# Where 62 reflections of an eigensolver stand beside two layers of a graph network, and who ends the second layer's LSTM

## The chip, the cores and the metric

The kernel runs as one launch on one core of a Trainium2 chip. The metric is the device time of that core in microseconds (us). The engines are TensorE (PE in the profile), VectorE (DVE), ScalarE (ACT), GpSimd (POOL) and SyncE (SP), and they work at the same time, tied together by semaphores.

## What is computed

The state `x` is 128 graphs of 64 nodes with 128 features (8192 tokens). Four layers are added to it, each behind a layer norm and a relu, all over the same 64x64 adjacency `adj`:

```python
h = jnp.maximum(_layernorm(x, axis=-1), 0.0)
x = x + _L0_gnn_ref(h, adj, ...)   # aggregate, W1, batch norm, relu, W2, batch norm
h = jnp.maximum(_layernorm(x, axis=-1), 0.0)
x = x + _L1_gnn_ref(h, adj, ...)   # two graph products, then four LSTMs over windows of 1, 2, 3, 4 nodes
h = jnp.maximum(_layernorm(x, axis=-1), 0.0)
x = x + _L2_gnn_ref(h, adj, ...)   # U.T, W1, relu, W2, U; U = eigenvectors of the normalised Laplacian
h = jnp.maximum(_layernorm(x, axis=-1), 0.0)
x = x + _L3_gnn_ref(h, adj, adj, ...)
```

The third layer needs `_, U = jnp.linalg.eigh(L_norm)` of a 64x64 matrix that depends on `adj` alone. The second layer's LSTMs are run over all windows of a node sequence, `i, f, g, o` being the four gates:

```python
c = sigmoid(f) * c + sigmoid(i) * tanh(gg)
h = sigmoid(o) * tanh(c)
```

## The kernel before, in words

The tokens are laid out as 4 quarters (`ITER`) of 4 chunks (`NK`) of 512 columns. The stages in time are the first layer (its first pass over 16 chunks, then its second over 8 pairs), a lead-in of the second layer for quarter 0, the LSTM for quarters 0 to 3, and the third and fourth layers, interleaved.

The eigenvectors come from a Householder reduction to tridiagonal form in 62 reflections, then a search for eigenvalues on a grid (two rounds), then a scan for each eigenvector (the code's "twist"), then a few 64x64 products. All of that is a serial chain on VectorE, with one or two small products on TensorE in each link. It is spread beside the first two layers. A reflection beside the first layer is `reflection_beside_l0` (lines 1386 to 1432): VectorE writes two columns into `NI`, TensorE multiplies them (`row_product`), GpSimd takes a square root, VectorE goes on, TensorE multiplies `S` by `vcol` (`av_product`), VectorE updates `S`. One such reflection stands in every step of the first layer's loop from step `FIRST_REFLECTED` on. A reflection beside the LSTM is `reflection` (from line 1453): it needs no GpSimd, sets its vector at L1494, sends TensorE one `av_product` (`small_product`), and takes it up at L1507. What else VectorE does there (adding the first layer's and the LSTM's results to the state at L2110, adding a bias at L2041, and the layer norms) is put between the reflection's instructions. Each link's small operations are also given to generators called `beside`, which a reflection advances by one item at each of its waits.

Nothing is scheduled on the chip. TensorE's order in the LSTM is written by a planner that counts its own clock: after each product it checks whether the next small product is due, and puts it there. `PACE_AV` is the distance between two reflections' products in that clock, `PACE_GRID` that of the two grid rounds, `PACE_TWIST` that of the scan. `beside_norm` adds to the pace while a quarter's layer norm is on VectorE. The planner's times are a layout, not a measurement. Once an instruction stands in TensorE's queue it waits there for its semaphore, and all behind it wait too.

The LSTM of a quarter has 11 rounds (`LSTM`; p is the window, s the step in it): rounds 0 and 1 are p = 1, rounds 2 and 3 p = 2, rounds 4 to 6 p = 3, rounds 7 to 10 p = 4. Each round is done for two sets q = 0, 1 of 1024 tokens, so there are two half rounds. In a half round TensorE makes 3 or 4 gates of 512, 336 or 256 columns, ScalarE takes their sigmoids and tanh (L1061), GpSimd forms the products (L1205), ScalarE takes tanh of the cell (L1085) and GpSimd the last product. In the last quarter the rounds from `ON_VECTOR` on have their products on VectorE (`last_rounds`, L2128), which is free only once the eigenvectors are done. In the same quarter ScalarE normalises quarters 0 and 1 for the third layer (L973, four instructions for each chunk) in the half rounds that `LAST_NORMED` names, between the gates and the tanh of the cell. Their statistics are `last_stats`, 92 small instructions on VectorE from a point in the planner's clock on.

At step 23 of the first layer VectorE also makes the aggregation matrices of the LSTM layer (`BIASES_AT`, L1993 to L1998), six instructions in a row between two reflections.

## Time and profile before

| what | us |
|---|---|
| median of 3 runs (896.1 to 898.14) | 897.49 |
| the profiled execution itself | 898.26 |
| its span in the trace | 896.5 |
| first layer | 0 to 155 |
| lead-in of the LSTM layer | 155 to 186 |
| LSTM, four quarters | 186 to 608 |
| third and fourth layer | 608 to 896 |
| TensorE busy, whole span | 792.7 (88%) |
| VectorE busy, whole span | 577.7 (64%) |
| ScalarE busy, whole span | 505.6 (56%) |
| GpSimd busy, whole span | 330.9 (37%) |

A row of the timeline gives the start in us, the duration in us, the engine, the line of the kernel, the operation, out<-in, shapes, and in brackets the time that the engine was idle before it and what ended that. TensorE's records come in two for each fp32 matmul, so "x6" are three matmuls. TensorE waits with the weight load and with the matmul; the matmul's wait is the one counted here, unless it is said otherwise. In the program's order below a matmul is one row.

### The profile page before, as it was taken

The page shows a single profiled execution, that of the slowest core. Times are in us where ns is not written, and L with a number is a line of the kernel's source. Part 1 is how long each engine was busy: PE and PEld are TensorE (multiplying, and loading weights), DVE is VectorE, ACT ScalarE, POOL GpSimd, SP SyncE. Part 2 cuts the span into 40 slices and gives each one's busy share as a digit, 9 for nine tenths or more (in the row PEclk, how much of TensorE's full clock was granted, in tenths as well). Part 3 has the DMA queues.
Part 4 walks back from the last instruction along what each step waited for, and adds up shares of the span by engine and source line. Part 5 has one row for each costly group of instructions (what it writes and reads, how often), then busy time and mean ns, then how long its engine had stood idle before and what let it go on. Part 6 is the DMA issues. An engine that isn't in the chain of part 4 may idle for free.

```text
span 896.5 us, 15860 instructions
## 1 busy us (share of the span) xinstructions
PE 792.7 (88%) x5323; PEld 520.6 (58%) x5323; DVE 577.7 (64%) x3091; ACT 505.6 (56%) x958; POOL 330.9 (37%) x490
## 2 busy tenths in 40 slices
PE   3867687799999999999799859999899999999998
PEld 1444334654688556864467524676748748747646
DVE  3899878799789997889997996646710720700101
ACT  2676575575766765675655634684654464434531
POOL 3556201376456655567555635300410220200000
PEclk9999798799999999999999979999999999999999
DMA  8000000000000000000000000000000100100101
GB/s 358 12 1 1 0 0 1 1 0 1 1 1 1 1 2 0 2 0 1 0 1 1 1 0 1 1 0 2 3 1 2 49 1 1 49 1 1 50 0 48
DMA packets 3409, 13.49 MB, mean 15 GB/s; under 512 B 512, under 2 KB 512, under 8 KB 2688
## 3 DMA queue, kind: packets, MB, share of 16 engines
q1 hardware_dynamic: 3328, 12.48, 3.5%
q8 instruction: 42, 0.69, 0.3%
q14 instruction: 39, 0.32, 0.1%
HBM read 8.28 MB, written 4.19 MB: 14 GB/s over the span
## 4 chain that ended last, share of the span: by engine, by line
PE 57%; DVE 26%; ACT 8%; POOL 5%; issue 3%; DMA 0%; DVEq 0%; SPq 0%; ACTq 0%; POOLq 0%
PE PS L525 56%; POOL BIG L1205 2%; ACT BIG L1061 2%; ACT T L1027 2%; DVE ST L1914 2%; DVE Fq L1693 1%; DVE seg L1694 1%; ACT T L973 1%; DVE X L2110 1%; DVE PS L1575 1%; DVE PS L1577 1%; DVE Z L1582 1%; DVE Z L1579 1%; ACT BIG L1085 1%; POOL sc L1145 1%
## 5 line engine op out<-in xcount | busy, mean ns | idle before, releaser
L525 PE MATMUL PS<-BIG,wts 128*128 128x512 f32 (+2 forms) x952 | 337.6, 497 | 8.3 <-ACT BIG L1061 5.0
L1205 POOL TENSOR_TENSOR BIG<-BIG 128x256 f32<-128x256 f32 (+2 forms) x220 | 210.3, 965 | 144.3 <-ACT BIG L1061 80.2
L525 PEld LDWEIGHTS PS<-BIG,wts 128*128 128x128 f32 x952 | 175.5, 191 | 131.2 <-issue 97.6
L1061 ACT ACTIVATE BIG<-PS,lbias 128x256 f32<-128x256 f32 (+2 forms) x312 | 162.0, 560 | 93.0 <-PE PS L525 90.9
L525 PE MATMUL PS<-H,wts 128*128 128x256 f32 (+2 forms) x312 | 111.3, 485 | 10.8 <-POOL H L1205 5.6
L965 ACT ACTIVATE BIG<-PS 128x1024 f32<-128x1024 f32 x64 | 64.7, 1024 | 85.4 <-PE PS L525 85.0
L525 PE MATMUL PS<-T,wts 128*128 128x512 f32 x192 | 104.8, 670 | 2.9 <-ACT T L965 2.5
L2155 DVE COPY T<-PS 128x256 f32<-128x256 f32 x32 | 12.2, 419 | 135.1 <-PE PS L525 135.1
L965 ACT ACTIVATE T<-PS 128x512 f32<-128x512 f32 (+1 forms) x96 | 48.3, 523 | 69.9 <-PE PS L525 69.7
L973 ACT ACTIVATE T<-X,shift,rstd 128x128 f32<-128x128 f32 x192 | 78.6, 483 | 10.3 <-POOL shift L1182 9.5
L525 PEld LDWEIGHTS PS<-H,wts 128*128 128x128 f32 x312 | 56.6, 193 | 45.7 <-issue 20.1
L2110 DVE TENSOR_TENSOR X<-X,PS 128x512 f32<-128x512 f32 x64 | 41.9, 680 | 61.7 <-PE PS L525 56.1
L1153 POOL TENSOR_SCALAR rstd<-mv 128x4 f32<-128x4 f32 x28 | 6.4, 228 | 190.6 <-DVE mv L1897 190.5
L1085 ACT ACTIVATE BIG<-BIG 128x512 f32<-128x512 f32 (+2 forms) x88 | 44.8, 509 | 53.1 <-POOL BIG L1205 52.8
L525 PE MATMUL PS<-wts,T 128*128 128x128 f32 (+1 forms) x384 | 62.1, 315 | 0.5 <-DVE T L2155 0.2
L525 PEld LDWEIGHTS PS<-wts,T 128*128 128x128 f32 x384 | 55.9, 194 | 8.5 <-issue 3.2
L525 PEld LDWEIGHTS PS<-wts,BIG 128*128 128x128 f32 x512 | 57.8, 192 | 1.9 <-issue 1.9
L525 PE MATMUL PS<-wts,BIG 128*128 128x128 f32 x512 | 57.8, 275 | 0.0
L525 PEld LDWEIGHTS PS<-T,wts 128*128 128x128 f32 x192 | 36.0, 208 | 34.8 <-issue 28.1
L1145 POOL TENSOR_TENSOR sc<-sc,cst 128x1 f32<-128x1 f32 x25 | 13.7, 547 | 69.2 <-DVE sc L1401 69.2
L525 PEld LDWEIGHTS PS<-S,vcol 128*128 128x128 f32 x124 | 20.8, 201 | 30.8 <-DVE S L1416 26.9
L525 PE MATMUL PS<-S,vcol 128*128 128x64 f32 (+61 forms) x124 | 24.2, 275 | 13.2 <-DVE S L1416 13.1
(334 smaller groups left out, 1215.5 us busy)
## 6 DMA issues: line engine op xcount, KB each, us to landing
X<-x_in SPq DMA_DIRECT2D x4, 1024.0 KB, 16.4
out<-X SPq DMA_DIRECT2D x16, 256.0 KB, 2.2
wts<-w_in SPq DMA_DIRECT2D x1, 3542.0 KB, 13.4
cst<-cst_in SPq DMA_DIRECT2D x1, 419.0 KB, 3.4
AA<-adj_in SPq DMA_DIRECT2D x2, 16.0 KB, 1.9
```

Source lines behind the costliest of these rows:

```text
L525: return nc.tensor.matmul(o, l, r, start=start, stop=stop)
L965: nc.scalar.activation(dst, src, fn, **kw).then_inc(act_done[k], 1)
L973: j = nc.scalar.activation(to[:, k, t * P:(t + 1) * P], X[:, a:a + P], ACT.Relu, bias=shifted[:, k, t:t + 1], scale=scale[:, k, t:t + 1])
L1027: j = nc.scalar.activation(T0[:, k, t * P:(t + 1) * P], X[:, a:a + P], ACT.Relu, bias=shift[:, k, t:t + 1], scale=rstd[:, k, t:t + 1])
L1061: nc.scalar.activation(LB[:, q, {"i": I_, "g": G_, "f": F_, "o": O_}[g], 0:n], PS[:, 3 * q + rank[q] % 3, 0:n], ACT.Tanh if g == "g" else ...
L1085: nc.scalar.activation(LB[:, q, I_, 0:n], LB[:, q, CELL, 0:n], ACT.Tanh).then_inc(act_set[q], 1)
L1145: return nc.gpsimd.tensor_tensor(o, ap, mh[:, 0:1] if e is None else e, ALU.pow)
L1205: nc.gpsimd.tensor_tensor(out, a, b, op).then_inc(pool_set[q], 1)
L1575: gop(v.scalar_tensor_tensor(ta, xn, d[:, i:i + 1], Z[:, up, :], ALU.add, ALU.mult))
L1914: v.bn_stats(ST1[:, h, c, :], Y1[:, h, c * CH:(c + 1) * CH]).then_inc(hidden_seen, 1)
L2110: v.tensor_tensor(x, x, src, ALU.add).then_inc(dve_done[k], 1)
L2155: v.tensor_copy(*graph_half(k, 1, to, side)).then_inc(dve_done[k], 1)
```

## The change

- `FIRST_REFLECTED` goes from 3 to 7: the first layer's steps 3 to 6 have no reflection, and the LSTM gets 41 in place of 37.
- The LSTM's layout is written anew: `PACE_AV` 5.9 to 5.4, `PACE_GRID` 49.0 and 41.5 to 48.5 and 38.5, `PACE_TWIST` 33.0 to 40.0.
- The six instructions of step 23 become a generator of its own, two of them beside the reflection of each of the steps 21, 22 and 23.
- The statistics for the normalisation of quarter 0 get tiles of their own (`rstd0`, `shift0`) and are taken early, in quarter 1's LSTM beside the biases of quarter 2, where the pace is 0.4 longer for 36 us of the planner's clock. Those of quarter 1 stay late (from 30.0 in place of 24.0 behind the last graph product).
- `ON_VECTOR` goes from 6 to 8: in the last quarter GpSimd also makes the products of rounds 6 and 7.
- `LAST_NORMED` moves the eight normalisations from rounds 6 to 9 (one in each half round) to rounds 8 to 10 (two in each half of round 8, one in each half of 9 and 10).

```diff
-ON_VECTOR = 6
-LAST_NORMED = {(6, 0): [(0, 0)], (6, 1): [(0, 1)], (7, 0): [(0, 2)], (7, 1): [(0, 3)],
-               (8, 0): [(1, 0)], (8, 1): [(1, 1)], (9, 0): [(1, 2)], (9, 1): [(1, 3)]}
+ON_VECTOR = 8
+LAST_NORMED = {(8, 0): [(0, 0), (0, 1)], (8, 1): [(0, 2), (0, 3)],
+               (9, 0): [(1, 0)], (9, 1): [(1, 1)], (10, 0): [(1, 2)], (10, 1): [(1, 3)]}
...
-FIRST_REFLECTED = 3
+FIRST_REFLECTED = 7
...
-BIASES_AT = L0_FIRST + 4
+MATRICES_AT = [L0_FIRST + 2, L0_FIRST + 3, L0_FIRST + 4]
...
-PACE_AV = 5.9
-PACE_GRID = [49.0, 41.5]
-PACE_TWIST = 33.0
+PACE_AV = 5.4
+PACE_GRID = [48.5, 38.5]
+PACE_TWIST = 40.0
...
-NORM_BESIDE, NORM_LASTS, LAST_NORMS = 1.4, 20.0, 24.0
+NORM_BESIDE, NORM_LASTS, LAST_NORMS = 1.4, 20.0, 30.0
+NORM_0 = (0.4, 36.0)
...
-                return any((j, 1, "turn") in there and clock[0] < there.get((j, NK - 1, "turn"), clock[0]) + NORM_LASTS
-                           for j in range(1, ITER))
+                for j in range(1, ITER):
+                    if (j, 1, "turn") in there and clock[0] < there.get((j, NK - 1, "turn"), clock[0]) + NORM_LASTS:
+                        return NORM_BESIDE
+                    if j == 2 and (0, NK - 1, "turn_h") in there and clock[0] < there[0, NK - 1, "turn_h"] + NORM_0[1]:
+                        return NORM_0[0]
+                return 0.0
...
+            def lstm_matrices():
...
+                dve.wait_ge(ld_w, 16)
+                made(v.tensor_scalar(tmp[:, :], PS[:, 7, 0:P], TINY, None, ALU.max))
+                yield
+                dve.wait_ge(prep_dve, done[0])
+                made(v.reciprocal(tmp[:, :], tmp[:, :]))
+                yield
+                made(v.tensor_scalar(BDR[:, :], BDAT[:, :], c1(0), None, ALU.mult))
+                yield
+                made(v.tensor_scalar(RB1[:, :], PS[:, 7, 0:P], W("bg1"), None, ALU.mult))
+                yield
...
+                if n in MATRICES_AT:
+                    beside = beside + [itertools.islice(matrices, 2)]
...
-                        yield from biases(i + 1)
+                        early = iter(())
+                        if i == 1:
+                            early = last_norm(0, rstd0, shift0, [there[0, NK - 1, "turn_h"] + 2.0], NORM_0[1] / 46)
+                        yield from merged(early, biases(i + 1))
                     else:
-                        yield from merged(last_stats(), behind)
+                        late = last_norm(1, rstd3, shift3, [there[i, NK - 1, "agg2"] + LAST_NORMS], LN_STEP)
+                        yield from merged(late, behind)
```

`last_norm` is `last_stats` for one quarter: 16 statistics, 16 aggregations, the roots and 4 shifts.

The instructions move on three engines. The first place is TensorE's queue in the first layer, steps 1 to 6 (`BDHT` is the aggregation, `T,wts` the product with W1, `NI,S` and `S,vcol` the two products of a reflection). Before:

```order
L525 MATMUL PS<-BDHT,T 128x128 x4
L525 MATMUL PS<-NI,S 128x65
L525 MATMUL PS<-T,wts 128x512 x2
L525 MATMUL PS<-S,vcol 128x64
L525 MATMUL PS<-BDHT,T 128x128 x4
```

After:

```order
L529 MATMUL PS<-BDHT,T 128x128 x4
L529 MATMUL PS<-T,wts 128x512 x2
L529 MATMUL PS<-BDHT,T 128x128 x4
L529 MATMUL PS<-T,wts 128x512 x2
L529 MATMUL PS<-BDHT,T 128x128 x4
L529 MATMUL PS<-NI,S 128x65
```

Five products with W1 now come ahead of the first reflection's row product, of which the piece shows the last two; before, one did.

The second place is TensorE's queue between the second grid round (`sc,cst`) and the scan's product (`both_ways`), in the last two quarters (`BIG,wts` and `H,wts` are gates, `BDR,T` a graph product, `cst,BIG` a transpose of the LSTM's result). Before:

```order
L525 MATMUL PS<-sc,cst 128x1
L525 MATMUL PS<-BDR,T 128x128 x4
L525 MATMUL PS<-BIG,wts 128x256 x8
L525 MATMUL PS<-BDR,T 128x128 x4
L525 MATMUL PS<-BIG,wts 128x256 x16
L525 MATMUL PS<-H,wts 128x512 x18
L525 MATMUL PS<-both_ways,cst 128x128
```

After:

```order
L529 MATMUL PS<-BIG,wts 128x256 x8
L529 MATMUL PS<-BDR,T 128x128 x4
L529 MATMUL PS<-BIG,wts 128x256 x16
L529 MATMUL PS<-H,wts 128x512 x18
L727 MATMUL PS<-cst,BIG 128x128 x4
L529 MATMUL PS<-H,wts 128x512 x3
L529 MATMUL PS<-BIG,wts 128x512 x3
L529 MATMUL PS<-H,wts 128x512
L529 MATMUL PS<-BIG,wts 128x512
L529 MATMUL PS<-both_ways,cst 128x128
```

The scan's product now stands behind eight more gates of 512 columns and a transpose; one graph product fewer stands between it and the grid round.

The third place is ScalarE's queue in round 8 of the last quarter (`BIG<-PS,lbias` are the four gates, `T<-X,shift,rstd` a normalisation, `BIG<-BIG` the tanh of the cell). Before:

```order
L1061 ACTIVATE BIG<-PS,lbias 128x256 x4
L973 ACTIVATE T<-X,shift,rstd 128x128 x4
L1085 ACTIVATE BIG<-BIG 128x256
L1061 ACTIVATE BIG<-PS,lbias 128x256 x4
L973 ACTIVATE T<-X,shift,rstd 128x128 x4
L1085 ACTIVATE BIG<-BIG 128x256
```

After:

```order
L1069 ACTIVATE BIG<-PS,lbias 128x256 x4
L981 ACTIVATE T<-X,shift,rstd 128x128 x8
L1093 ACTIVATE BIG<-BIG 128x256
L1069 ACTIVATE BIG<-PS,lbias 128x256 x4
L981 ACTIVATE T<-X,shift,rstd 128x128 x8
L1093 ACTIVATE BIG<-BIG 128x256
```

Each half of round 8 now has two normalisations ahead of its tanh; rounds 6 and 7 have none, and round 10 has one in each half.

## Rows read from the trace of the kernel before

**Rows 1.** Timeline of PE in the first layer's first pass
```profile
40.56 0.43 PE L525 MATMUL PS<-NI,S 128*128 128x62 f32 x2 [0.94 <-DVE NI L1395]
40.83 1.94 PE L525 MATMUL PS<-T,wts 128*128 128x512 f32 x4
...
45.68 0.43 PE L525 MATMUL PS<-NI,S 128*128 128x61 f32 x2 [0.94 <-DVE NI L1395]
```

**Rows 2.** Timeline of ACT in the same steps
```profile
42.80 1.26 ACT L990 ACTIVATE BIG<-PS,wts 128x512 f32<-128x512 f32 x2 [0.94 <-PE PS L525]
44.78 0.60 ACT L965 ACTIVATE T<-PS 128x512 f32<-128x512 f32 x1 [0.72 <-PE PS L525]
```

**Rows 3.** Timeline of PE about step 23 of the first layer
```profile
128.46 0.42 PE L525 MATMUL PS<-NI,S 128*128 128x45 f32 x2 [2.60 <-DVE NI L1395]
128.70 4.52 PE L525 MATMUL PS<-T,wts 128*128 128x512 f32 x6
...
134.72 2.82 PE L525 MATMUL PS<-T,wts 128*128 128x512 f32 x6
```

**Rows 4.** Timeline of DVE there, the longest of the six
```profile
125.94 0.95 DVE L1994 RECIPROCAL tmp<-tmp 128x128 f32<-128x128 f32 x1
```

**Rows 5.** Instructions of L1512, one for each reflection but the last (min/median/max)
```profile
L1512 DVE SCALAR_TENSOR_TENSOR urow<-xrow,sc,PS x36: 200/226/244, 171.1 to 384.5; 128x37 f32<-128x37 f32 x1, 128x36 f32<-128x36 f32 x1, 128x35 f32<-128x35 f32 x1, 128x34 f32<-128x34 f32 x1
```

**Rows 6.** Waits of DVE, 186 to 391 us (total us, times, longest)
```profile
DVE sc L1507 <- PE PS L525: 15.6, 19, 2.5
```

**Rows 7.** Waits of PE's weight loads in the same stretch
```profile
PEld PS L525 <- DVE S L1494: 4.3, 8, 0.8
```

**Rows 8.** Timeline of DVE, the reflections' take-up of their products
```profile
199.76 0.21 DVE L1507 TENSOR_SCALAR sc<-PS,sc 128x1 f32<-128x1 f32 x1
...
227.53 0.22 DVE L1507 TENSOR_SCALAR sc<-PS,sc 128x1 f32<-128x1 f32 x1 [1.38 <-PE PS L525]
...
286.92 0.22 DVE L1507 TENSOR_SCALAR sc<-PS,sc 128x1 f32<-128x1 f32 x1 [0.67 <-PE PS L525]
...
292.11 0.22 DVE L1507 TENSOR_SCALAR sc<-PS,sc 128x1 f32<-128x1 f32 x1 [0.24 <-PE PS L525]
```

**Rows 9.** Timeline of DVE at the second grid round
```profile
489.80 0.22 DVE L1658 SCALAR_TENSOR_TENSOR sc<-PS,sc 128x1 f32<-128x1 f32 x1 [3.88 <-PE PS L525]
```

**Rows 10.** Timeline of PE at the scan's product
```profile
531.50 0.79 PE L525 MATMUL PS<-both_ways,cst 128*128 128x128 f32 x2 [8.79 <-DVE both_ways L1718]
...
532.94 4.04 PE L525 MATMUL PS<-H,wts 128*128 128x512 f32 x6
```

**Rows 11.** Timeline of ACT in rounds 8 to 10, last quarter
```profile
588.63 1.64 ACT L973 ACTIVATE T<-X,shift,rstd 128x128 f32<-128x128 f32 x4
590.17 0.40 ACT L1085 ACTIVATE BIG<-BIG 128x256 f32<-128x256 f32 x1
...
594.06 0.40 ACT L1085 ACTIVATE BIG<-BIG 128x256 f32<-128x256 f32 x1
...
604.27 0.42 ACT L1085 ACTIVATE BIG<-BIG 128x256 f32<-128x256 f32 x1
...
607.84 0.42 ACT L1085 ACTIVATE BIG<-BIG 128x256 f32<-128x256 f32 x1
```

**Rows 12.** Timeline of PE, round 7 of the last quarter
```profile
581.43 2.86 PE L525 MATMUL PS<-H,wts 128*128 128x256 f32 x12 [1.78 <-DVE H L2128]
...
587.09 0.70 PE L525 MATMUL PS<-H,wts 128*128 128x256 f32 x2 [1.26 <-ACT BIG L1061]
```

**Rows 13.** Timeline of POOL, products and how long they take
```profile
544.07 1.27 POOL L1205 TENSOR_TENSOR H<-BIG 128x512 f32<-128x512 f32 x1 [0.74 <-ACT BIG L1085]
...
570.75 0.90 POOL L1205 TENSOR_TENSOR BIG<-BIG 128x336 f32<-128x336 f32 x1 [0.59 <-ACT BIG L1085]
```

**Rows 14.** Timeline of DVE, one operation twice, beside POOL and not
```profile
544.34 1.04 DVE L1844 TENSOR_TENSOR lnv<-lnv 128x16 f32<-128x16 f32 x1
...
545.89 0.17 DVE L1844 TENSOR_TENSOR lnv<-lnv 128x16 f32<-128x16 f32 x1
```

More of the change, by code:

```diff
@@ L374, in build @@
         shift3 = sb("shift3", [P, NK, TPC])
+        rstd0 = sb("rstd0", [P, NK, TPC])
+        shift0 = sb("shift0", [P, NK, TPC])
         T0 = sb("T0", [P, NK, CH])
@@ L1082, in _ @@
                                 norm_tiles(j, k, "norm", j * NK + k + 1, C_PE.at(ITER - 1, "agg2"),
[L1083 removed]
+                                           *((T3, rstd3, shift3) if j else (T0, rstd0, shift0)), by=[last_norms] * NK)
                         act.wait_ge(pool_set[q], R_POOL.at(i, f"c{r}" if s else f"ig{r}"))
@@ L2048, in biases, with last_norm @@
                         bias(i, k)
-                def last_stats():
-                    at = [there[ITER - 1, NK - 1, "agg2"] + LAST_NORMS]
+                def last_norm(j, scale, to, at, step):
                     def later():
-                        busy(0.2)
-                        at[0] += LN_STEP
+                        busy(0.17)
+                        at[0] += step
                         return at[0]
                     for k in range(NK):
-                        dve.wait_ge(act_done[k], C_ACT.at(ITER - 1, "norm"))
-                    for j, scale, to in ((0, rstd, shift), (1, rstd3, shift3)):
-                        for k in range(NK):
-                            dve.wait_ge(dve_done[k], C_DVE.at(j, "add_h"))
-                            for t in range(TPC):
-                                a = j * SG + k * CH + t * P
-                                do(v.bn_stats(stats[:, k, t, :], X[:, a:a + P]))
-                                yield later()
-                        wait()
-                        for k in range(NK):
-                            for t in range(TPC):
-                                do(v.bn_aggr(mv[:, k, t, :], stats[:, k, t, :]))
-                                yield later()
-                        wait()
-                        yield from norm_roots(do, wait, later, scale)
-                        for k in range(NK):
-                            v.scalar_tensor_tensor(to[:, k, :], mv[:, k, :, 0], -1.0, scale[:, k, :], ALU.mult, ALU.mult)\
-                                .then_inc(last_norms, 1)
-                            yield later()
@@ new lines, in last_norm @@
+                        dve.wait_ge(dve_done[k], C_DVE.at(j, "add_h"))
+                        for t in range(TPC):
+                            a = j * SG + k * CH + t * P
+                            yield later()
+                            do(v.bn_stats(stats[:, k, t, :], X[:, a:a + P]))
+                    yield later()
+                    wait()
+                    for k in range(NK):
+                        for t in range(TPC):
+                            yield later()
+                            do(v.bn_aggr(mv[:, k, t, :], stats[:, k, t, :]))
@@ L2080, in first_add @@
+                    yield later()
+                    wait()
+                    yield from norm_roots(do, wait, later, scale)
+                    for k in range(NK):
+                        v.scalar_tensor_tensor(to[:, k, :], mv[:, k, :, 0], -1.0, scale[:, k, :], ALU.mult, ALU.mult)\
+                            .then_inc(last_norms, 1)
+                        yield later()
                 def first_add(k):
```

24 lines of the change are left out of this document (13 added, 11 removed).

## The prediction, written before the result

> **What bounds the kernel now.** I read stage by stage, since a busy share of the whole span mixes stages with different limits. In the first layer the timeline shows TensorE idle 0.94 us once in each step, waiting for VectorE's two columns of the next reflection, and the same row product comes again 5.12 us later [rows 1]: the step is paced by the reflection's chain. In the LSTM TensorE is nearly always busy, and the question is who of the two is late. Over the reflections VectorE waited 15.6 us for products that TensorE sent late [rows 6], and TensorE waited 4.3 us for VectorE [rows 7]. So there TensorE sets the end, with the chain close behind. At the scan it is the other way: TensorE stood 8.79 us with the scan's product at the head of its queue [rows 10]. In the last rounds ScalarE's normalisation stands between gates and tanh [rows 11], and TensorE waits for what follows from it [rows 12]. The third and fourth layers aren't touched.
>
> **First layer, steps 3 to 6.** Without a reflection a step goes around W1's product (1.94 us), ScalarE's copy of its result (1.26), ScalarE's copy of the next aggregation (0.60) and back to W1's product [rows 1, 2]: 3.80, with three or four hand-overs 3.95 us. The next aggregation on TensorE runs beside the first copy, and GpSimd's layer norm beside all of it. Against 5.12 us that is 1.17 less, in four steps **-4.7 us**. Ends: nothing less than 3.80 (-5.3), and one step in which TensorE's clock drops. Such a drop is seen at step 23: behind an idle time of 2.60 us six records took 4.52 us, and 2.82 us elsewhere [rows 3], 1.7 us more. In the short steps nothing would hide it (-3.0).
>
> **Step 23's matrices.** Six instructions in a row kept the reflection's columns back: TensorE waited 2.60 us, and the 1.7 us of slow clock came behind it [rows 3], less 0.2 us of wait that every step has: 4.1 us. Spread out two by two they still take VectorE's time, the reciprocal 0.95 us [rows 4] and five of 0.2 to 0.3 us, 2.2 us in all, and the reflection sets the step here too, so I count all of it. TensorE's gaps become short, and the slow clock should go: **-1.9 us** (between 0, if the clock still drops, and -4.1, if the slots hide them). The 21 reflections that stay are four elements longer, **+0.4 us**.
>
> **The LSTM: four more reflections, set closer.** Before, 36 take-ups lie between 171.1 and 384.5 us, 213.4 us for 35 intervals [rows 5]. Without its waits [rows 6] VectorE needed 197.8 us. Each more costs what a quiet one does, 292.11 - 286.92 - 0.24 = 4.95 us [rows 8], a little less beside other work: 4.9, and 19.6 for four. The norm of quarter 0, moved in here, costs what the norm of quarter 1 did: four intervals from 199.76 to 227.53, less 1.38 us of waiting [rows 8], are 26.4 us; less four reflections and one addition of 0.6 that leaves 6.2 us. VectorE's need becomes 197.8 + 19.6 + 6.2 = 223.6 us.
> TensorE's own time was 213.4 - 4.3 = 209.1 us. Counted in its order, the last of the 41 products stands behind 5.9 us more of matmuls than the last of the 37 did (1.2 us are the added small products, the rest LSTM). That is 215.0 us. So VectorE is 8.6 us late if it never idles. It will idle where TensorE is late anyway (2 to 3 us of the 15.6 are such places), so TensorE waits some 11 us, where it waited 4.3. With the added products themselves: **+6.8 and +1.2 us**. What each wait holds up is all of TensorE's queue, the gates first, and with them ScalarE and GpSimd. Bounds: +2 if VectorE hides half of it in the waits of the rounds (ScalarE and GpSimd are late there too), +11 if each interval falls badly.
>
> **Grid rounds.** The first is bound by VectorE before and after. In the second VectorE waited 3.88 us for its product [rows 9], which now comes 3.4 us earlier in TensorE's order: the slack is used up and nothing is gained. **0** (0 to +1).
>
> **The scan.** From the take-up at 489.80 [rows 9] to 531.50 [rows 10] VectorE worked 41.7 us, TensorE 41.7 - 8.8 = 32.9. In the new order TensorE has eight 512-column matmuls and a transpose more before the scan's product and a graph product less, at 0.86 us for one of 512 columns (2.82 us hold three, with the first one's start [rows 3]) 6.9 + 0.5 - 0.9 = 6.5 us: 39.4. VectorE has one addition (0.6) and some ten norm instructions (1.2) more: 43.5. The wait goes from 8.8 to 4.1: **-4.7 us**. Behind the wait six records took 4.04 us [rows 10], 1.2 more than the 2.82 of the same size [rows 3]; half of that should go, **-0.6**.
>
> **The last rounds.** The norms leave rounds 6 and 7, where TensorE waited 1.78 and 1.26 us [rows 12]: -3.0. GpSimd takes some 0.3 us longer for a product that the next round waits for (0.90 us for 336 columns [rows 13]), once or twice: +0.3. In round 8 a half takes gates, two norms of 1.64 us and a tanh of 0.40 on ScalarE. With one norm it took 594.06 - 590.17 = 3.89 us [rows 11]. ScalarE is full in it (four gates are about 1.7), so two make about 5.35: +2.9 for two halves. Round 10 had none and took 607.84 - 604.27 = 3.57 [rows 11]; one in each half adds 0.3, and the last stands ahead of the last tanh, for which the third layer waits: +1.7. Sum **+1.9 us**. The tail of small products has less norm work beside it: **-0.3**.
>
> **The sum.** First layer -4.7 - 1.9 + 0.4 = -6.2 us. LSTM 6.8 + 1.2 + 0 - 4.7 - 0.6 + 1.9 - 0.3 = +4.3 us. Together -1.9 us on the profiled execution's own 898.26, which is 0.8 above the median of the runs. I take 0.5 to 1 us off for waits that overlap: a TensorE that waits for VectorE lets ScalarE and GpSimd catch up, and their waits shrink. That is about -2.7 us, 895.6 on the profiled execution and **894.8 us** on the median of 897.49.
>
> **A rule against it.** One small operation took 1.04 us when it began beside a product of GpSimd that ran 1.27 us from 544.07, and 0.17 us two steps later [rows 13, 14]. The Trainium skill ("SBUF — State Buffer", section "Who interferes with whom") says that a VectorE instruction with two inputs in SBUF and a GpSimd instruction that reads SBUF block each other for a whole instruction, whoever starts first. The trace agrees in this pair. By that rule the moved norm's eleven two-input operations, in a stretch where GpSimd works, could each meet such a block: eleven times 0.87 us, 9.6 us in place of the 6.2 taken from the trace, and 3.4 us more in the sum.
>
> **The rivals.**
> *VectorE keeps up.* The reflections need about as much as before between products, because the waits for TensorE were spread where they can be used; TensorE's waits stay near 4 to 6 us. For it: 15.6 us of slack were there, and every single wait of TensorE was under 0.9 us [rows 6, 7]. Against it: the counts leave VectorE 8.6 us short. Then 4 to 6 us less than my sum, 889 to 891 us.
> *VectorE becomes the bound (slower).* One mechanism, in quarters 0 to 2 of the LSTM: additions, biases and norms fall on intervals with no slack, and each delay goes to TensorE's queue undiminished, because the next products are due at once. Price: intervals of 5.9 to 7 us against 5.3, in three norm stretches and three rows of additions, +11 us and over in place of 6.8, with the blocked operations on top +3; the scan still waits. It decides the sign once TensorE's waits for VectorE in the reflections pass about 14 us. 898 to 903, most likely 900.
> *The first layer gives little.* The clock drops in the short steps and at the matrices: 3 us of the 6.2 are lost, 897.5 us, no change.
>
> **Chances.** Forecast 0.45 (891.5 to 897), VectorE keeps up 0.2, VectorE the bound 0.2, little from the first layer 0.15. A measurement of this kernel can tell about 0.2%, 1.8 us, from no change. Below 895.7: the second case and most of the first, 0.56. Above 899.3: most of the third, 0.17. Between: 0.27. The range, 888.5 to 901 us, takes in the second case and most of the third.
>
> **What would show it.** First layer: W1's products 3.9 to 4.0 us apart in steps 3 to 6, and the layer over at 149 in place of 155 us. Step 23: no wait of 2.6 us and no 4.52 us. LSTM: TensorE's waits for the reflections' vector near 11 us with VectorE's waits for TensorE under 5 us. Scan: a wait of about 4 us. Round 8: tanh to tanh 5.3 us. The LSTM from its first product to its end some 3 to 4 us longer. The prediction is wrong if TensorE's waits in the reflections stay at 5 or go past 14, or if the clock falls in the short steps.

## The result, and the profile after

The changed kernel takes **908.07 us** (median, 907.40 to 912.86), the kernel before 896.80 on the same chip; the ratio is 1.0132, interval 1.0113 to 1.0151. It is 11.3 us slower where I forecast 2.7 us faster, and it lies outside the range. The first layer did better than forecast, the LSTM 15 us worse. The profiled execution is the slowest of the four, 4.8 us above the median; between the two traces lie 14.6 us, so some 3 us of what the rows below show are not in the medians.

**First layer.** The timeline of TensorE after, steps 2 to 6 (start, duration, engine, line, operation, out<-in, shapes, idle before and who ended it), answers to [rows 1]:

```profile
25.58 1.96 PE L529 MATMUL PS<-T,wts 128*128 128x512 f32 x4 [0.93 <-ACT T L973]
29.38 1.98 PE L529 MATMUL PS<-T,wts 128*128 128x512 f32 x4 [0.95 <-ACT T L973]
33.21 1.98 PE L529 MATMUL PS<-T,wts 128*128 128x512 f32 x4 [0.69 <-ACT T L973]
37.10 1.98 PE L529 MATMUL PS<-T,wts 128*128 128x512 f32 x4 [0.69 <-ACT T L973]
40.92 1.55 PE L529 MATMUL PS<-T,wts 128*128 128x512 f32 x3 [0.52 <-ACT T L973]
```

W1's products are 3.80 to 3.89 us apart, where they were 5.12, and what they wait for is ScalarE's copy. The six instructions for the matrices, spread over steps 21 to 23, leave no wait behind (the same timeline, which answers to [rows 3]):

```profile
116.84 0.42 PE L529 MATMUL PS<-NI,S 128*128 128x50 f32 x2 [0.35 <-DVE NI L1403]
117.10 2.81 PE L529 MATMUL PS<-T,wts 128*128 128x512 f32 x6
121.45 0.42 PE L529 MATMUL PS<-NI,S 128*128 128x49 f32 x2 [0.36 <-DVE NI L1403]
121.71 2.81 PE L529 MATMUL PS<-T,wts 128*128 128x512 f32 x6
125.89 0.42 PE L529 MATMUL PS<-NI,S 128*128 128x48 f32 x2 [0.29 <-DVE NI L1403]
```

The 2.60 us and the record of 4.52 us are gone. The first product with the LSTM's matrix (`BDP`) came at 161.5 us before and comes at 153.0 now: 8.5 us gained, 6.2 forecast.

**LSTM.** From the first product of a reflection beside the LSTM to the third layer's first product it took 438.2 us before and takes 458.0. The stages after (stretch: length, busy us and count of PE, its loads, DVE, ACT and POOL, granted clock, DMA share, GB/s): the reflections, then to the grid's second product, to the scan, to the vector `V`, to the end:

```profile
160.99:400.54 239.55, 223.57 (x1002) 153.56 (x1001) 223.55 (x1556) 144.71 (x283) 132.37 (x138) 0.98 0.00 1
400.54:456.07 55.53, 47.23 (x163) 25.02 (x162) 52.65 (x234) 37.24 (x71) 36.17 (x30) 1.00 0.00 1
456.07:543.04 86.97, 76.05 (x293) 50.00 (x293) 79.96 (x336) 49.06 (x95) 52.34 (x56) 0.96 0.00 1
543.04:563.00 19.96, 16.13 (x44) 8.61 (x44) 17.83 (x90) 6.92 (x13) 8.57 (x8) 0.84 0.00 1
563.00:619.02 56.02, 47.60 (x189) 33.77 (x189) 19.82 (x60) 37.29 (x90) 17.00 (x20) 0.97 0.00 0
```

The same five stretches of before:

```profile
170.20:389.26 219.06, 209.54 (x963) 145.29 (x964) 195.71 (x1369) 139.35 (x273) 127.87 (x132) 1.00 0.00 1
389.26:444.39 55.13, 49.27 (x164) 26.57 (x163) 52.00 (x237) 35.77 (x69) 35.43 (x31) 0.97 0.00 1
444.39:531.50 87.11, 70.37 (x295) 47.48 (x293) 77.03 (x337) 50.73 (x103) 51.97 (x57) 0.96 0.00 1
531.50:548.30 16.80, 14.94 (x40) 7.69 (x40) 14.25 (x85) 4.75 (x7) 6.29 (x5) 0.88 0.01 2
548.30:608.40 60.10, 55.17 (x213) 37.77 (x213) 31.76 (x122) 42.56 (x101) 14.45 (x15) 0.97 0.00 1
```

Counted by these stages the whole loss stands in the first line: 239.6 us in place of 219.1. That line also holds 39 records of matmuls more, 16 of them the added reflections', and the last line 24 fewer, so part of the LSTM's work has moved forward with the chain's later end. VectorE's busy time rose in the first line by 27.8 us, and the granted clock fell from 1.00 to 0.98 of full speed. Who waited for whom between the reflections (total us, times, longest), weight loads of TensorE and take-ups of VectorE, answers to [rows 6, 7]:

```profile
PEld PS L529 <- DVE S L1502: 23.0, 17, 3.6
DVE sc L1515 <- PE PS L529: 7.1, 11, 2.5
```

TensorE waited 23.0 us for VectorE, where it had waited 4.3 and I forecast about 11. VectorE waited 7.1, where I had counted 2 to 3. The worst place is the end of the first quarter (timeline of TensorE, and below it two take-ups of VectorE):

```profile
212.68 2.72 PE L529 MATMUL PS<-BIG,wts 128*128 128x512 f32 x8
218.47 0.64 PE L529 MATMUL PS<-S,cst 128*128 128x32 f32 x2 [3.08 <-DVE S L1502]
...
219.35 3.71 PE L529 MATMUL PS<-BIG,wts 128*128 128x336 f32 x6
```

```profile
209.37 0.22 DVE L1515 TENSOR_SCALAR sc<-PS,sc 128x1 f32<-128x1 f32 x1 [0.37 <-PE PS L529]
219.58 0.22 DVE L1515 TENSOR_SCALAR sc<-PS,sc 128x1 f32<-128x1 f32 x1
```

A layer norm stands between these two take-ups, so they are 10.2 us apart, VectorE never idles for a product, and TensorE stands 3.08 us with the gates of the next round behind the waiting product. The norm's instructions alone don't make the interval so long. VectorE's timeline inside it shows four small operations that ran long, below one that didn't, and the second fence GpSimd's products beside them:

```profile
210.80 0.17 DVE L1849 TENSOR_TENSOR lnv<-lnv 128x16 f32<-128x16 f32 x1
...
211.97 1.25 DVE L1849 TENSOR_TENSOR lnv<-lnv 128x16 f32<-128x16 f32 x1
...
213.49 0.96 DVE L1852 TENSOR_TENSOR lnv<-lnv 128x16 f32<-128x16 f32 x1
...
214.61 1.19 DVE L1855 SCALAR_TENSOR_TENSOR lnv<-lnv 128x16 f32<-128x16 f32 x1
...
216.60 1.20 DVE L1890 SCALAR_TENSOR_TENSOR shift<-mv,rstd 128x16 f32<-128x16 f32 x1
```

```profile
211.93 3.84 POOL L1213 TENSOR_TENSOR BIG<-BIG 128x512 f32<-128x512 f32 x3 [1.47 <-ACT BIG L1069]
216.50 2.12 POOL L1213 TENSOR_TENSOR BIG<-BIG 128x512 f32<-128x512 f32 x2 [0.74 <-ACT BIG L1093]
```

The first row began with GpSimd idle and took 0.17 us. Each of the other four began while a product of GpSimd ran (one of 512 columns takes some 1.27 us) and ended as that product did. Together they make the interval about 3.9 us longer, more than the 3.08 us that TensorE stood; no run takes them away, so what the wait would be without them is an estimate. Over all reflections ten small operations are longer by 0.4 us or more than is usual for them, 8.3 us together, where the kernel before has five with 4.4 us (three of them, 2.8 us, in its longest interval, of 8.2 us).

Behind TensorE's wait the clock fell to half (the windows there):

```profile
217.50:218.40 0.90, 0.00 (x0) 0.00 (x0) 0.86 (x5) 0.78 (x3) 0.90 (x2) 0.95 0.00 0
218.40:225.10 6.70, 6.63 (x19) 5.08 (x20) 5.89 (x42) 4.80 (x12) 2.00 (x3) 0.50 0.01 2
225.10:227.00 1.90, 1.90 (x11) 1.42 (x10) 0.00 (x0) 1.90 (x6) 0.00 (x0) 0.99 0.00 0
```

**Scan and last rounds.** TensorE after, answering to [rows 10, 12], and the last wait:

```profile
543.04 0.80 PE L529 MATMUL PS<-both_ways,cst 128*128 128x128 f32 x2 [4.16 <-DVE both_ways L1726]
...
544.67 5.10 PE L529 MATMUL PS<-H,wts 128*128 128x512 f32 x6
...
588.15 0.70 PE L529 MATMUL PS<-H,wts 128*128 128x256 f32 x2 [1.92 <-POOL H L1213]
...
598.28 0.70 PE L529 MATMUL PS<-H,wts 128*128 128x256 f32 x2 [1.71 <-ACT BIG L1069]
603.71 0.70 PE L529 MATMUL PS<-H,wts 128*128 128x256 f32 x2 [1.71 <-ACT BIG L1069]
...
619.02 2.09 PE L529 MATMUL PS<-BDU,T 64*64 64x64 f32 x124 [2.50 <-ACT BIG L1093]
```

ScalarE in rounds 8 and 9 after, answering to [rows 11] (the two norms of a half are the 3.17 us, one norm is 1.63):

```profile
597.47 0.40 ACT L1093 ACTIVATE BIG<-BIG 128x256 f32<-128x256 f32 x1
...
599.82 3.17 ACT L981 ACTIVATE T<-X,shift,rstd 128x128 f32<-128x128 f32 x8
602.89 0.41 ACT L1093 ACTIVATE BIG<-BIG 128x256 f32<-128x256 f32 x1
...
605.25 1.63 ACT L981 ACTIVATE T<-X,shift,rstd 128x128 f32<-128x128 f32 x4
```

The scan's wait is 4.16 us, as forecast, and tanh to tanh in round 8 is 5.42 (5.3 forecast). The six records behind the scan's product took 5.10 us, longer than the 4.04 of before. In round 7 one wait of 1.92 us is left, and it is for a product of GpSimd.

### The profile page after: what moved, and what is told of

Same layout as the page of the kernel before. It is cut to its first block, busy times and chain, and to the rows that moved or that the text cites. A ratio compares the mean times of both kernels' runs of the same rounds, so it can differ in the third digit from the quotient of the medians.

```text
span 911.1 us, 15929 instructions
## 1 busy us (share of the span) xinstructions
PE 798.9 (88%) x5323; PEld 522.9 (57%) x5323; DVE 589.6 (65%) x3151; ACT 507.0 (56%) x958; POOL 339.1 (37%) x498
## 4 chain that ended last, share of the span: by engine, by line
PE 52%; DVE 35%; ACT 5%; issue 4%; POOL 2%; DMA 0%; DVEq 0%; SPq 0%; ACTq 0%; POOLq 0%
PE PS L529 52%; DVE X L2137 2%; ACT T L981 2%; DVE Fq L1701 1%; DVE ST L1922 1%; DVE seg L1702 1%; DVE PS L1583 1%; DVE PS L1585 1%; DVE Z L1590 1%; DVE Z L1587 1%; DVE Z L1628 1%; ACT BIG L1069 1%; DVE stats L1877 1%; ACT T L1035 1%; DVE Z L1623 1%
## 5 line engine op out<-in xcount | busy, mean ns | idle before, releaser
L1213 POOL TENSOR_TENSOR BIG<-BIG 128x256 f32<-128x256 f32 (+2 forms) x230 | 218.8, 960 | 161.7 <-ACT BIG L1069 93.5
L529 PE MATMUL PS<-H,wts 128*128 128x256 f32 (+2 forms) x312 | 115.4, 501 | 11.5 <-POOL H L1213 6.2
L529 PE MATMUL PS<-T,wts 128*128 128x512 f32 x192 | 101.8, 652 | 5.8 <-ACT T L973 5.6
L529 PEld LDWEIGHTS PS<-H,wts 128*128 128x128 f32 x312 | 58.9, 199 | 47.5 <-issue 22.6
L981 ACT ACTIVATE T<-X,shift,rstd 128x128 f32<-128x128 f32 x192 | 78.3, 482 | 11.7 <-POOL shift L1190 10.9
L973 ACT ACTIVATE T<-PS,wts 128x512 f32<-128x512 f32 x32 | 21.9, 686 | 20.6 <-PE PS L529 20.6
```

Of the source, the lines that this page charges most:

```text
L529: return nc.tensor.matmul(o, l, r, start=start, stop=stop)
L973: nc.scalar.activation(dst, src, fn, **kw).then_inc(act_done[k], 1)
L981: j = nc.scalar.activation(to[:, k, t * P:(t + 1) * P], X[:, a:a + P], ACT.Relu, bias=shifted[:, k, t:t + 1], scale=scale[:, k, t:t + 1])
L1213: nc.gpsimd.tensor_tensor(out, a, b, op).then_inc(pool_set[q], 1)
```

## The experiments

**Method.** Each kernel is timed beside the kernel before, whose median lay between 896.8 and 897.4 us every time. The executions of one kernel scatter by 1 to 2.5 us (standard deviation), so a difference of 2 us or less between two medians below is at the edge of what can be told. Where the text says "the matrices alone", it is the first run below, 893.93 us. Four parts are told apart: A, the matrices spread over three steps; B, four reflections moved, at a pace of 5.4; C, the norms (quarter 0's statistics early, `ON_VECTOR`, `LAST_NORMED`); D, the paces of the grid rounds and the twist.

### Which part

A alone, on the kernel before: the block at `BIASES_AT` out, `MATRICES_AT` and `lstm_matrices` in.

> The kernel before with one part of the change: the six instructions for the LSTM's matrices spread two by two over three steps of the first layer. In the changed kernel the steps from the second pass's second row product to its seventh took 27.0 us against 29.4 before, and the wait of 2.60 us and the record of 4.52 us are gone. Theory (the spreading is a gain by itself and reaches the end undiminished): 2 to 4 us less, 893 to 895. Rival (the gain in the first layer came from the steps without a reflection alone): 896 to 897.5.

893.93 us, ratio 0.9953 (0.9937 to 0.9970). The first layer ends 2.2 us earlier and the LSTM keeps its 438.2 us to the tenth. The theory held; this is faster than both kernels.

A and B:

```diff
-FIRST_REFLECTED = 3
+FIRST_REFLECTED = 7
-PACE_AV = 5.9
+PACE_AV = 5.4
```

> The kernel before with the matrices spread and with four more reflections moved from the first layer to the LSTM, paced at 5.4; norms, grid and twist paces as before. Theory (the closer reflections are what makes the changed kernel slow: VectorE can't keep up, whatever the norms do): the first layer gives 8 us, the reflections cost 14 to 16, 901 to 905. Rival (the norms are to blame: the norm of quarter 0 moved between the reflections, and two norms in a half of round 8): the reflections cost 5 to 8, 893 to 897.

912.76 us, ratio 1.0170 (1.0144 to 1.0197): 18.8 us over A alone, more even than the theory said. The first layer gave 5.3 us, the LSTM took 21.6 more. With the norms and paces of before, part B is as bad as in the changed kernel, and worse. So B, four more reflections at the closer pace, is the cause, and C and D together make it better by 4.7. How much of B is the pace is asked further down.

A and D (on the first run: `PACE_GRID` 48.5 and 38.5, `PACE_TWIST` 40.0):

> The kernel before with the matrices spread and the new paces of the grid rounds and the twist (48.5, 38.5 and 40.0 in place of 49.0, 41.5 and 33.0): neither the four reflections nor the norms are moved. Theory (TensorE's wait at the scan falls from 8.8 to about 4 us and the rest of the LSTM only has that much less to do later): 4 to 5 us less than with the matrices alone, 889 to 891. Rival (what fills the wait is missing as cover in the last rounds, which wait longer in its place): within 1.5 us of the matrices alone.

895.32 us, ratio 0.9983 (0.9967 to 0.9998): 1.4 over A alone. The theory fell, the rival held. TensorE's scan wait of 7.78 us is gone altogether, and here nothing is gained by it. The stretches from the grid's second product to the scan and on to `V`, with A alone and with A and D:

```profile
441.74:528.88 87.14, 71.80 (x294) 48.12 (x292) 77.05 (x337) 51.17 (x103) 52.01 (x57) 0.96 0.00 1
528.88:545.41 16.53, 14.64 (x41) 7.67 (x41) 14.25 (x85) 4.75 (x7) 6.29 (x5) 0.90 0.00 1
```

```profile
438.18:523.17 84.99, 76.48 (x305) 50.62 (x303) 78.82 (x341) 51.16 (x103) 51.30 (x57) 0.96 0.00 1
523.17:543.29 20.12, 14.70 (x44) 7.03 (x42) 19.96 (x91) 7.29 (x11) 10.88 (x9) 0.88 0.00 1
```

Together they are 105.1 us in place of 103.7. VectorE is the one that is always busy here (98.8 of 105.1 us). What TensorE does in the wait are graph products, and they bring VectorE their additions ahead of `V`: its busy time rises by 7.5 us. What is missing in the last rounds then (TensorE's work there, at full clock, is 4.0 us less) gives only 0.3 us back: its idle time and its slow clock grow by 1.0 and 2.7.

A, C and D, without B (the changed kernel with `FIRST_REFLECTED = 3` and `PACE_AV = 5.9`):

> The changed kernel with three steps without a reflection and a pace of 5.9, as before: so 37 reflections beside the LSTM, while the matrices, the norms, the grid and twist paces are the changed ones. Theory (closer reflections are to blame): first layer 4.7 us longer than in the changed kernel, the LSTM 14 to 16 shorter, 896 to 899. Rival (the norms are to blame): LSTM 4 to 6 us shorter at most, 906 to 909.

895.29 us, ratio 0.9970 (0.9956 to 0.9984): 12.8 us less than the changed kernel. The theory held in kind and was a little short in size: 0.7 us under its range, with an LSTM 16.6 us shorter (14 to 16 forecast) and a first layer 5.1 us longer (4.7 forecast). Two numbers, `FIRST_REFLECTED` and `PACE_AV`, make the changed kernel's whole loss and a little more.

A and C (the last run with the paces of before):

> The changed kernel with 37 reflections at 5.9 and the grid and twist paces of before: so the matrices spread and the norms moved (quarter 0's early, two in a half of round 8), nothing else. The run with the changed paces as well took 895.3 us. Theory (VectorE has room for the early norm between 37 reflections, and ScalarE's two norms in round 8 cost what rounds 6 and 7 give): within 1.5 us of the matrices alone, 892.5 to 895.5. Rival (the moved norms shorten the last rounds by 2 to 4 us once VectorE has room): 890 to 892.

902.51 us, ratio 1.0049 (1.0029 to 1.0068). Neither was right: 8.6 us over A alone, 7.2 over A, C and D. The scan's wait is 9.87 us here and none with D; the length from the first reflection to the scan is 367.8 against 365.9. So the paces D are worth nothing by themselves, and 7 us once the norms are moved. In the traces the LSTM is 6.2 us shorter with D (the table below), and 5.0 of these lie behind `V`, where TensorE has 15 records fewer left to do (A and C, then A, C and D):

```profile
551.90:614.11 62.21, 53.80 (x207) 38.30 (x207) 22.68 (x74) 41.82 (x99) 22.09 (x25) 0.94 0.00 1
```

```profile
550.25:607.47 57.22, 49.59 (x192) 34.99 (x193) 20.54 (x63) 38.05 (x92) 17.94 (x21) 0.95 0.00 1
```

Here, other than with A alone, what TensorE does ahead of `V` comes off the end. Why it does so only with the norms moved, no run tells. (The traced executions lie 2.7 and 4.5 us above their medians.)

### Is it VectorE's work, or where the products stand?

One instruction more on VectorE in each reflection, on A alone:

```diff
                 need(op(v.tensor_scalar(hd, x0, beta, guard, ALU.mult, ALU.max)))
+                op(v.memset(added[:, :], 0.0))
                 need(op(v.reciprocal(nc_, hd)))
```

> The kernel with the matrices spread (37 reflections beside the LSTM), and one instruction more in each of them on VectorE: a fill of 128x512 elements of a tile that nothing reads, ahead of the reciprocal. TensorE has no product more. An instruction of 512 columns should take 0.3 to 0.7 us, so VectorE gets 11 to 25 us more work. Theory (from the first product beside the LSTM on, VectorE's work sets the time, so that added work reaches the end nearly whole): four fifths or more of what the fills take, 903 to 914. Rival (TensorE sets it, and VectorE has the 15.6 us that it waited for products): the fills take up those waits first, at most 5 us more than the matrices alone, 894 to 899.

The fills took 0.485 us each:

```profile
L1498 DVE MEMSET added<- x37: 485/485/485, 158.1 to 393.6; 128x512 f32 x37
```

Between the first and the last take-up VectorE's need rose from 197.8 to 215.4 us, 17.6 more, and the kernel by 9.8, to 903.71 (ratio 1.0072, 1.0056 to 1.0089). The time lies in the theory's range, but the share doesn't: a little over half of the work reached the end, where the theory wanted four fifths and the rival at most 5 us. (Not all of the 17.6 are the fills: small operations that ran long beside GpSimd, as in the interval above, grew from 4.4 to 7.7 us.) VectorE's waits for products fell from 15.7 to 7.8 us. **Of 15.7 us of waits only 7.9 could be used.** The rest lie where the next product isn't sent yet however late VectorE is elsewhere. This is the assumption that my sum rested on, and it is half wrong.

The reverse: VectorE's additions cut from 512 columns to one, with A and B and with A alone.

```diff
-                x = X[:, i * SG + k * CH:i * SG + (k + 1) * CH]
-                v.tensor_tensor(x, x, src, ALU.add).then_inc(dve_done[k], 1)
+                x = X[:, i * SG + k * CH:i * SG + k * CH + 1]
+                v.tensor_tensor(x, x, src[:, 0:1], ALU.add).then_inc(dve_done[k], 1)
```

(and the bias in the same way)

> The kernel with the matrices spread and the four reflections moved at a pace of 5.4 (912.8 us), and in it VectorE's additions to the state and of the bias beside the LSTM cut from 512 columns to one; 24 of them fall between the reflections, 0.68 us each before, so 14 us of VectorE's work there are gone and as much again later. That leaves part of the computation out. TensorE's products and their order are the same. Theory (VectorE's work sets the time): the part with the reflections 10 to 14 us shorter, the grid rounds and the scan 5 to 8, in all 893 to 898. Rival (the four reflections cost because each holds up TensorE's queue once more, whatever else VectorE does): 4 us less at most, 908 to 912.

> The kernel with the matrices spread and 37 reflections, with the same additions on VectorE cut from 512 columns to one as in the run with 41 reflections, where that took 16.2 us off: the control for it. That leaves part of the computation out. Theory (with 37 reflections TensorE sets the time between them, where it waited 4.4 us for VectorE, and only the grid rounds and the scan follow VectorE): 5 to 9 us less than the matrices alone, 885 to 889. Rival (VectorE sets the time with 37 as with 41): 14 us less or more, at most 880.

With 41 reflections it takes 16.2 us off (896.54), with 37 it takes 4.4 off (889.51). The same work costs VectorE nearly four times as much time at the end with 41 as with 37. Ratios 1.0001 (0.9983 to 1.0018) and 0.9909 (0.9891 to 0.9926). The first theory held; the second missed its range by 0.5 us, 4.4 us off where it wanted 5 at least. So VectorE's work is what the four reflections at the closer pace make dear: at 37 and 5.9 TensorE sets the time, at 41 and 5.4 VectorE does for most of the way.

### The pace

37 reflections at a pace of 5.4 (on A alone), and 41 at 5.0 (on A and B):

> The kernel with the matrices spread, 37 reflections beside the LSTM as before, paced at 5.4 in place of 5.9: the closer setting without the four added reflections. Theory (VectorE's work sets the time, and it is the same): within 2 us of the matrices alone, 892 to 896. Rival (it is the closer setting that costs, since TensorE then waits at the head of its queue): 5 us more or over, 899 to 905.

> The matrices spread and the four reflections moved, paced at 5.0 in place of 5.4. At 5.4 VectorE still waited 8.8 us for products between the first and the last take-up. Theory (VectorE's own work is what counts, and the waits that remain lie where the order of TensorE bunches its matmuls): VectorE's waits fall to 3 to 5 us, the last product comes 4 to 5 us earlier, and most of that is lost later; 909 to 912. Rival (the pace was too wide, and set closer the reflections hide): 898 to 905.

901.51 us (ratio 1.0054, 1.0032 to 1.0075) and 902.13 (1.0049, 1.0030 to 1.0069). Both theories fell and both rivals held. Set closer, 37 cost 7.6 us more with VectorE's need unchanged (196.5 against 197.8), and 41 cost 10.6 less. So VectorE's need alone doesn't explain the time either. Of the 18.8 us that B costs over A alone, 7.6 come with the closer pace by itself, and 11.2 when the four reflections are added at that pace. No run has 41 reflections at 5.9, so whether the closer pace was needed for them isn't shown. The weight loads' waits for the reflections' vector, first A alone, then 37 at 5.4:

```profile
PEld PS L525 <- DVE S L1494: 4.4, 8, 0.8
```

```profile
PEld PS L525 <- DVE S L1494: 18.4, 16, 2.6
```

At 5.4 less of the LSTM stands between two products, TensorE comes to them sooner than VectorE does, and stops there. The chain then ends sooner (`V` 10.3 us earlier, counted from the first product beside the LSTM), and what is left of the LSTM behind `V` takes 76.8 in place of 60.4 us.

The intervals between VectorE's take-ups show what a single pace can't follow. Each number is a start less the start before it, with what VectorE waited for the product split off behind a "+" (0.2 us or more). The first 24 intervals:

```
37 at 5.9 (A alone)   5.5 6.2 5.8 5.5 6.2 7.0 6.2 8.2 5.0+1.4 5.0+2.5 5.0+1.4 5.0+0.2 5.0+1.1 5.0+0.2
                      5.0+0.3 5.8+0.3 6.4 5.5 4.9+0.7 4.9+0.2 5.3 6.2 7.2 6.2
41 at 5.4 (changed)   5.5 6.2 5.6 5.6 5.5 6.6 6.9 5.6+0.4 10.2 5.1+2.5 5.1+0.2 5.0+0.2 5.0+0.5 5.0+0.6
                      5.0+0.2 4.9 6.1 5.5 5.5 5.5 4.9 5.0 5.3 5.4
41 at 5.0 (A and B)   5.5 6.2 5.6 5.0 6.1 5.5 7.1 6.0 8.9 5.7 5.3+0.7 5.0 4.9 5.0
                      5.0 4.9 4.9 5.6 5.5 5.5 5.5 4.9 4.9 4.9
```

A quiet reflection needs 4.9 to 5.0 us, one with additions 5.5 to 6.2, and a norm makes single intervals of 7 to 10. In quiet stretches VectorE waits for products that a pace of 5.4 or 5.9 sends late, and in norm stretches TensorE waits for VectorE. Each is late in its turn, and the waits of one don't pay for those of the other. At 5.0 VectorE's waits fall to 2.7 us (8.8 at 5.4), and the last product comes 10.7 us earlier.

The changed kernel at 5.0:

> The changed kernel paced at 5.0 in place of 5.4, nothing else. With the norms of before that took 10.6 us off. Theory (at 5.4 the order makes VectorE and TensorE late in turn: VectorE waited 7.1 us for products, TensorE 23.0 for vectors; at 5.0 the products are always in time): VectorE's waits under 3 us, the last product 8 to 10 us earlier, 898 to 903. Rival (VectorE's need of 226.6 us sets the end and the norm of quarter 0 adds to it, so the pace gives little): 905 to 909.

910.72 us (ratio 1.0149, 1.0126 to 1.0172). VectorE's waits do fall, to 1.2 us, and `V` comes 13.9 us earlier in the LSTM, but the stretch behind it is 14.1 us longer. The theory's waits came, its gain did not; the rival was nearer. With C and D in place the same step that took 10.6 us off gives nothing.

### How the cost sets in

One and two reflections more in the first layer, and one and two more beside the LSTM (`FIRST_REFLECTED` 2, 1, 4, 5, on A alone, each with a pace that makes the reflections take about as long together):

> The matrices spread, and one reflection the other way: two steps of the first layer without a reflection in place of three, so 36 beside the LSTM, paced at 6.05 so that they take as long. Theory (a reflection beside the LSTM costs 3 to 5 us, as the four did, and 1.2 in the first layer): 1 to 3 us less than the matrices alone, 891 to 893. Rival (with 37 VectorE hides, so one less only lets it wait longer): 1 to 2 us more, 895 to 896.

> As the last, with one step without a reflection: 35 beside the LSTM, paced at 6.2. The second step of the first layer also has VectorE's work for the Laplacian, so the step may be longer. Theory (each costs 3 to 5 us beside the LSTM): 889 to 893. Rival (they hide): 896 to 900.

> The matrices spread and one reflection moved beside the LSTM (38 of them), paced at 5.75 so that they take as long as 37 at 5.9. Theory (from 37 on VectorE's need of about 4.9 us for each goes to the end, less 1.2 in the first layer): 3 to 4 us over the matrices alone, 897 to 898. Rival (each order of TensorE has its own luck): anything, such as under 894 or over 901.

> As the last with two reflections moved (39) and a pace of 5.65. Theory: 6 to 9 us over the matrices alone, 900 to 903. Rival: no regular step from the last run.

| kernel | reflections, pace | median us | VectorE's need | TensorE for its vector | TensorE's waits in all | LSTM |
|---|---|---|---|---|---|---|
| a_fr1 | 35, 6.2 | 895.34 | 192.0 | 2.7 | 64.3 | 439.1 |
| a_fr2 | 36, 6.05 | 897.45 | 194.9 | 5.2 | 65.1 | 440.0 |
| a_matrices | 37, 5.9 | 893.93 | 197.8 | 4.4 | 66.3 | 439.4 |
| a_fr4 | 38, 5.75 | 897.72 | 203.8 | 9.5 | 70.9 | 442.8 |
| a_fr5 | 39, 5.65 | 899.79 | 209.2 | 13.4 | 75.9 | 446.9 |
| ab_50 | 41, 5.0 | 902.13 | 215.8 | 26.7 | 80.5 | 450.7 |
| ab_both | 41, 5.4 | 912.76 | 220.5 | 20.6 | 85.6 | 461.3 |
| changed | 41, 5.4 | 908.07 | 226.6 | 23.0 | 79.0 | 459.0 |
| after_50 | 41, 5.0 | 910.72 | 221.1 | 28.7 | 84.0 | 459.7 |
| a_pace54 | 37, 5.4 | 901.51 | 196.5 | 18.4 | 73.6 | 445.4 |
| ac_norms | 37, 5.9 | 902.51 | 203.7 | 4.4 | 73.2 | 448.6 |
| ad_matpace | 37, 5.9 | 895.32 | 197.7 | 4.3 | 64.6 | 440.0 |
| after_fr3 | 37, 5.9 | 895.29 | 203.5 | 4.4 | 65.7 | 442.4 |

"Need" is first to last take-up without VectorE's waits for products; "in all" sums the weight loads' waits for any other engine from 7 us behind the first `BDP` product to the third layer (without "issue"); the LSTM is that same stretch.

Below 37 the LSTM gets no shorter: TensorE sets it, and one and two reflections fewer gave 3.5 and 1.4 us more in the whole, not less (theory of both wrong; the rival was 1.5 us under for 36, and 35 lies just under its range). From 37 on each adds 3.4 and 4.1 us to the LSTM, and 3.8 and 2.1 to the whole (that theory held for 38; 39 lies 0.2 us under its range). So in the LSTM's column the hinge lies at the number that the kernel before had. The whole time can't place it as well: 36 gave as much more as 38, and 2.6 us of its 3.5 stand, in the traces, in the third and fourth layer (290.5 us against 288.0), whose code no run here changes. Count and pace also change together in this series, and it doesn't tell one from the other.

The table's last two columns go together: from a_matrices to the changed kernel TensorE's waits grow by 12.7 us and the LSTM by 19.6. The waits for one thing alone don't do it: ab_50 waits longer for the reflections' vector than ab_both, and is 10.6 us faster.

## Why the prediction was wrong

**First layer: right, and small in size against what happened later.** Steps 3 to 6: 3.80 to 3.89 us apart, forecast 3.95. Matrices: forecast -1.9; alone they gave 2.2 us in the trace of a_matrices, and 3.4 on the median. 8.5 us in all for 6.2.

**VectorE's need: 226.6 us for 223.6.** Four reflections cost 22.7 (ab_both against a_matrices), not 19.6. The moved norm cost 6.1 (changed against ab_both), forecast 6.2. The price from the trace held for it (2.8 of the 6.1 us are small operations that ran long beside GpSimd), and the 9.6 us that the rule on two-input operations would have made of it ("SBUF — State Buffer", section "Who interferes with whom", in the Trainium skill) did not come. The blocks that the rule tells of are in the trace, but only some of the operations met one.

**"It will idle where TensorE is late anyway (2 to 3 us of the 15.6 are such places)": this step failed.** It idled 7.1 us. The run with the fills shows it by itself: of 15.7 us of waits 7.8 stay even when VectorE has 17.6 us more to do. I took a difference of two totals, 223.6 less 215.0, for the wait. Two engines that hand a product back and forth lose in each interval what the later one is late, and those losses add up over intervals in which it is now the one and now the other. Need and idle time together make 233.7 us between the take-ups, where my sum had about 226. TensorE's wait for the vector grew by 18.7 us (4.3 to 23.0), where the sum had **+6.8** (4.3 to about 11). Of the 12 us that were missing, 3.0 are VectorE's need, 4.6 its idle time, and 4.3 are TensorE's own time, which came to 210.7 us (233.7 less 23.0) and not to 215.0, since its other waits had shrunk.

**The clock in the reflections: not in the sum.** In the changed kernel the reflections' stretch lost 5.1 us of full clock, before none. The clock fell twice there, for 6.8 us at the gap of 3.08 us and for 3.4 us at one of 1.97 us.

**"A TensorE that waits for VectorE lets ScalarE and GpSimd catch up": right, and larger.** In the stretch with the reflections TensorE's waits for them fell from 17.2 to 9.4 us; I had taken 0.5 to 1 off. That these waits fell because the others rose is argued; the run only shows both.

**Scan: the wait as forecast (4.16 for 4.1), the gain not shown.** With the norms of before (ad_matpace), filling this wait gave VectorE more to do ahead of `V`, and of the -4.7 and -0.6 nothing came. With the norms moved the same paces took 7.2 us off (ac_norms against after_fr3). No run leaves D alone out of the changed kernel, so what the -4.7 was worth in it stays open. From the first grid product to `V` TensorE's weight loads waited 33.2 us for other engines there, in place of 35.7. The -0.6 didn't come: the six records behind the scan's product took 5.10 us, and the clock was at half there.

**Last rounds: right in rounds 8 and 10, wrong in round 7.** 5.42 for 5.3 us in round 8, 3.89 for 3.87 in round 10 (tanh at 614.58 and at 618.47), a last wait of 2.50 for 1.13. But the -3.0 for the norms that leave rounds 6 and 7 came as -1.1: of the waits of 1.78 and 1.26 us one is gone, and in place of the other TensorE waits 1.92 us for GpSimd's product, which `ON_VECTOR = 8` had taken from VectorE; the +0.3 for it was too small. TensorE's idle time behind `V` rose from 4.9 to 8.4 us, 3.5 where the sum had +1.9.

**The rivals.** "VectorE becomes the bound" is what happened. Its condition was TensorE's wait past 14 us, measured 23.0, and its mechanism the intervals with norms and additions, "no slack" and "each delay goes to TensorE's queue undiminished". Its price, 11 us and over, was still too low for the 18.7 measured, and the result lies 5 us above its own 898 to 903. What stood against it in the prediction were the 15.6 us of slack and single waits under 0.9 us; the first was worth half its face. Its blocked operations, +3, are seen too: 8.3 us in place of 4.4 over the reflections.

**What stays open.** Of the LSTM's 19.8 us, 10.9 are TensorE's waits, 5.1 slow clock and 1.2 the added products; 2.6 I can't place. Why the step from 5.4 to 5.0 is worth 10.6 us with the norms of before and nothing with the moved ones, and why the paces D are worth 7.2 us with C and -1.4 without it, is not settled: each run is another order of some 1,700 matmul records, and I haven't separated the order from what it does to single waits. Nor did any run test a pace that follows each interval's own need, or 41 reflections at the pace of before, or the norms placed where GpSimd leaves the small operations alone.

## What to carry to other kernels

A total of waits is not slack. Before giving an engine more to do because it waits, put extra work of a known size on it, spread in the same way: here 17.6 us more cost 9.8, and that one run would have shown that four reflections at 4.9 us each can't hide. Where two engines hand a product to and fro at a fixed distance, compare the distance with the need interval by interval, since a mean that fits them all together is too wide for some and too close for others. And don't book a wait of one engine inside another's serial chain (the scan) as a gain before a run has filled it: what fills it may give the chain more work, and the same filling was worth nothing in one layout here and 7 us in another.

## What the runs showed of the hardware

TensorE's granted clock fell from 1.00 to 0.50 (of 2.4 GHz, so 1.2) at about 218.4 us, at the end of 3.08 us without a matmul, and stayed there for 6.7 us; in that stretch TensorE was busy 6.63 us and did what takes half as long. A wait of 3 us cost about 6.4 in all. The kernel before had none in the whole 219 us of its reflections.

A layer norm's small operation of VectorE with two inputs (128x16 or less), begun beside a running product of GpSimd (`TENSOR_TENSOR`), waited for the product's end: four of them took 0.96 to 1.25 us, where 0.17 us is usual. In the changed kernel all 18 that began so took over 0.3 us and ended 0.02 to 0.04 us behind the product, and none of the other 56 took as long; in the kernel before 12 of 14, and none of the other 60.

Four matmuls of the third layer's first product start late for no reason that the profile shows, in the changed kernel

```profile
622.96 0.33 PE L529 MATMUL PS<-BDU,T 64*64 64x64 f32 x4 [1.86 <-issue]
```

and in seven of the other kernels (1.30 to 1.58 us), not in the kernel before nor in a_matrices. In the changed kernel it came with slow clock behind it (eight matmuls of 512 columns took 4.72 us, before 3.60), and the two together are most of the 4.0 us by which the third and fourth layers are longer there, with code that the change doesn't touch. It is one profiled execution, and the slowest of its kernel, so a part of it is not in the median.
